# Ternary feed-forward block: scaling and low parts of the second token half on VectorE instead of GpSimd, at the end of the first half

## The chip, the cores and the metric

One core of one Trainium2 chip (trn2) runs the whole program. The time is that of the device, in microseconds from one launch, as the median of several runs. The profiler's span, from the first to the last instruction, is about 2 us shorter than the time of the execution that it belongs to.

## The reference

Two post-norm decoder layers on 8 sequences of 100 tokens with 512 channels (800 tokens). Each layer has a mixer or attention, a cross attention on 361 context rows and a feed-forward block, each followed by x = layernorm(x + block(x)). The change lies in the feed-forward block of the first layer, whose weights are made ternary:

```python
def _L0_ffn_ref(x, w1, b1, w2, b2):
    def _bit_quant(w):
        scale = jnp.maximum(jnp.mean(jnp.abs(w)), EPS)
        w_ternary = jnp.clip(jnp.round(w / scale), -1.0, 1.0)
        return w + jax.lax.stop_gradient(w_ternary - w)
    w1q = _bit_quant(w1)
    w2q = _bit_quant(w2)
    h = jnp.einsum('bsd,fd->bsf', x, w1q) + b1
    h = jax.nn.gelu(h, approximate=False)
    return jnp.einsum('bsf,df->bsd', h, w2q) + b2

def _layernorm(x, axis=-1, eps=1e-05):
    m = jnp.mean(x, axis=axis, keepdims=True)
    v = jnp.var(x, axis=axis, keepdims=True)
    return (x - m) / jnp.sqrt(v + eps)
...
    x = _layernorm(x + _L0_xattn_ref(x, ctx_2048, ...), axis=-1)
    x = _layernorm(x + _L0_ffn_ref(x, L0_ffn_w1, L0_ffn_b1, L0_ffn_w2, L0_ffn_b2), axis=-1)
```

w1 is 2048 x 512 and w2 is 512 x 2048.

## The kernel before

The program is a chain of stages, each a block with one instruction list per engine and a barrier of all engines behind it. Activations lie in `X` as 128 partitions x C = 4 channel groups x 800 tokens. In the ternary stage (`ternary_ffn_stage`, L1198) the tokens are done in two halves of 400 (`at` = 0 and 1), and each half in FC = 16 steps `j`, one per 128 hidden channels. The order on each engine is written out by hand, and semaphores tie the engines together.

- **TensorE** (L1284 to L1305): `hidden(at, j)` is 8 matmuls (L1255; 4 channel groups, high and low part of X), `down(at, j)` is 8 matmuls (L1268; 4 output groups, high and low part of the hidden values). The list runs hidden 0, hidden 1, then down j and hidden j + 2 in turn. So down j stands behind hidden j + 1. In the first half hidden j waits for `up_ready` and down j for `down_ready`, as the ternary weights are made while the half runs; every down waits for `h2_ready`.
- **ScalarE** (L1318 to L1341): in each step Gelu out of PSUM into `hid` (L1322) and its high part (Copy, L1325). Between the steps stand pieces of the layer norm and the high parts of the second half (`high_part`, L1309).
- **VectorE** (L1368 to L1405): in each step the low part `h2` (L1381, one 128x400 tensor_tensor), and, in the first half only, the ternary weights of a later step: `ternary_up(j + 2)` and `ternary_down(j + 1)`, each a tensor_scalar of 128x512 (L1350, L1359) and a scalar_tensor_tensor of 128x512 (L1352, L1361). In the first half the layer norm of the second half's tokens is done in between: `nrm.center(1, i)` in steps 0 and 1, `nrm.invert(1, i)` (a reciprocal of 128x200, L195) in steps 6 and 8. At the end of the first half VectorE waits for `y_all` and adds the four outputs into X (`add_out`, L1365), which `down(1, 0)` waits for.
- **GpSimd** (L1408): has six instructions in this stage. They are the second half's `nrm.apply(1, i)` (L204, two tensor_tensor of 128x800: X = centred values x 1/std) and its low parts, four tensor_tensor of 128x400 (L1413), each behind the high part that ScalarE made. `hidden(1, 0)` waits for all of them through `part_lo`.

The low parts of the first half are made by VectorE at the stage's head, in the same form (L1373). SyncE's list fetches the ternary weights' raw values into a ring of 8 places and is told by `up_ready` and `down_ready` when a place is free.

Of the kernel before, what the change touches and what calls it, by code (L numbers as in the profile page):

```python
# [17 lines left out]
ACT = mybir.ActivationFunctionType  # L18
ALU = mybir.AluOpType
# [5 lines left out]
C = D // P  # L25
# [415 lines left out]
FC = F // P  # L441
# [756 lines left out]
def ternary_ffn_stage(nc, core, a, tern, early):  # L1198


    X, psum = core.X, core.psum
    LEAD, nrm, half = 2, tern.nrm, core.half
    with ExitStack() as ctx:
        def sb(name, shape, dt=F32):
            return ctx.enter_context(nc.sbuf_tensor(f"tf_{name}", shape, dt))
# [7 lines left out]
        parts = sb("parts", [P, 2, C, N], F32R)  # L1213
        S_ = {n: core.sem(f"tf_{n}") for n in (
            "part_hi", "part_lo", "last_mean", "up_low", "down_low", "up_ready", "down_ready", "h_mm", "hid_ready", "hi_ready", "h2_ready", "y_all", "y_out")}
        core.held += [*tern.sems, *tern.raw_in]
        block = ctx.enter_context(nc.Block())

        def piece(j):

            r = j % tern.SLOTS
            whole = tern.first[:, r, :] if r < tern.LEAD else ring[:, r - tern.LEAD, :]
            return whole, whole[:, 0:D].rearrange("p (c o) -> p c o", c=C), whole[:, D:2 * D]

        def half_of(h):
            return slice(h * HALF, (h + 1) * HALF)

        def quarter(i):
            return slice(i * QUARTER, (i + 1) * QUARTER)

        def cols(j):
            return slice(j * P, (j + 1) * P)

        def last_mean_at(i):
            return psum[:, (4, 7)[i], quarter(i)]

        @block.sync
        def _(sp):
            for j in range(tern.LEAD, FC):
                if j >= tern.SLOTS:  # L1240
                    sp.wait_ge(S_["up_ready"], j - tern.SLOTS + 1)
                    sp.wait_ge(S_["down_ready"], j - tern.SLOTS + 1)
                tern.fetch(sp, a, j, piece(j)[0])
            early.fetch(sp, a)
# [61 lines left out]

        @block.scalar
        def _(act):
            def high_part(at, c):  # L1309
                act.wait_ge(nrm.normed, 2 * at + 2)  # L1310
                act.activation(parts[:, 0, c, half_of(at)], X[:, c, half_of(at)], ACT.Copy).then_inc(S_["part_hi"], 1)

            act.wait_ge(nrm.normed, 1)
            act.activation(parts[:, 0, :, quarter(0)], X[:, :, quarter(0)], ACT.Copy)
            act.wait_ge(nrm.normed, 2)
            for c in range(C):
                act.activation(parts[:, 0, c, quarter(1)], X[:, c, quarter(1)], ACT.Copy).then_inc(S_["part_hi"], 1)
            for at in range(2):  # L1318
                for j in range(FC):
                    m, r = at * FC + j, j % 2  # L1320
                    act.wait_ge(S_["h_mm"], m + 1)
                    act.activation(hid[:, r, :], psum[:, 4 + r, 0:HALF], ACT.Gelu,  # L1322
                                   bias=core.param("b1", j)).then_inc(S_["hid_ready"], 1)
                    act.wait_ge(S_["hid_ready"], m + 1)
                    act.activation(h2[:, r, 0, :], hid[:, r, :], ACT.Copy).then_inc(S_["hi_ready"], 1)  # L1325
                    if not at and j in (1, 2):
                        nrm.square(act, 1, j - 1)
                    if not at and j == 4:
                        nrm.root(act, 1, 0)
                        nrm.root(act, 1, 1)  # L1330
                    if not at and j in (10, 11, 12, 13):
                        high_part(1, j - 10)
                    if at and j in (3, 4):
                        nrm.square(act, 2, j - 3)
                    if at and j == 7:
                        nrm.root(act, 2, 0)
                        nrm.root(act, 2, 1)
            for i in range(2):
                nrm.square(act, 3, i)
            for i in range(2):  # L1340
                nrm.root(act, 3, i)  # L1341

        @block.vector
        def _(dve):
            def ternary_up(j):
                _, up, _ = piece(j)
                dve.wait_ge(tern.raw_in[j % tern.SLOTS], 16 * (j // tern.SLOTS + 1))
                if j:
                    dve.wait_ge(S_["up_ready"], j)
                dve.tensor_scalar(low_up[:, :, :], up, half[:, 1:2], None, ALU.is_lt).then_inc(S_["up_low"], 1)  # L1350
                dve.wait_ge(S_["up_low"], j + 1)
                dve.scalar_tensor_tensor(w_up[:, :, cols(j)], up, half[:, 0:1], low_up[:, :, :],  # L1352
                                         ALU.is_gt, ALU.subtract).then_inc(S_["up_ready"], 1)

            def ternary_down(j):
                _, _, down = piece(j)
                if j:
                    dve.wait_ge(S_["down_ready"], j)
                dve.tensor_scalar(low_down[:, :], down, half[:, 3:4], None, ALU.is_lt).then_inc(S_["down_low"], 1)  # L1359
                dve.wait_ge(S_["down_low"], j + 1)  # L1360
                dve.scalar_tensor_tensor(w_down[:, j, :], down, half[:, 2:3], low_down[:, :],  # L1361
                                         ALU.is_gt, ALU.subtract).then_inc(S_["down_ready"], 1)

            def add_out(at, c, tok):
                dve.scalar_tensor_tensor(X[:, c, tok], psum[:, c, tok.start - at * HALF:tok.stop - at * HALF],  # L1365
                                         core.param("b2", c), X[:, c, tok], ALU.add, ALU.add).then_inc(S_["y_out"], 1)

            nrm.apply(dve, 0, 1)  # L1368
            dve.wait_ge(tern.half_ready, 4)
            ternary_up(0)  # L1370
            for c in range(C):
                dve.wait_ge(S_["part_hi"], c + 1)
                dve.tensor_tensor(parts[:, 1, c, half_of(0)], X[:, c, half_of(0)], parts[:, 0, c, half_of(0)],  # L1373
                                  ALU.subtract).then_inc(S_["part_lo"], 1)
            ternary_up(1)
            ternary_down(0)
            for at in range(2):
                for j in range(FC):
                    m, r = at * FC + j, j % 2
                    dve.wait_ge(S_["hi_ready"], m + 1)  # L1380
                    dve.tensor_tensor(h2[:, r, 1, :], hid[:, r, :], h2[:, r, 0, :], ALU.subtract).then_inc(S_["h2_ready"], 1)  # L1381
                    if not at and j + LEAD < FC:
                        ternary_up(j + LEAD)
                    if not at and j + 1 < FC:
                        ternary_down(j + 1)
                    if not at and j in (0, 1):
                        nrm.center(dve, 1, j)
                    if not at and j in (6, 8):
                        nrm.invert(dve, 1, (j - 6) // 2)
                    if at and j in (3, 4):  # L1390
                        nrm.center(dve, 2, j - 3)
                    if at and j in (8, 9):
                        nrm.scale(dve, 2, j - 8)
                dve.wait_ge(S_["y_all"], at + 1)
                if at == 0:
                    for c in range(C):
                        add_out(0, c, half_of(0))
            for i in range(2):
                for c in range(C):
                    add_out(1, c, nrm.tok(3, i))  # L1400
            for i in range(2):
                tok = nrm.tok(3, i)
                dve.wait_ge(S_["last_mean"], i + 1)
                dve.tensor_tensor(nrm.cen[:, :, tok], X[:, :, tok], last_mean_at(i).unsqueeze(1).broadcast_to([P, C, QUARTER]),
                                  ALU.subtract).then_inc(nrm.cen_ready, 1)  # L1405

        @block.gpsimd
        def _(pool):  # L1408
            for i in range(2):
                nrm.apply(pool, 1, i)  # L1410
            for c in range(C):
                pool.wait_ge(S_["part_hi"], C + c + 1)
                pool.tensor_tensor(parts[:, 1, c, half_of(1)], X[:, c, half_of(1)], parts[:, 0, c, half_of(1)],  # L1413
                                   ALU.subtract).then_inc(S_["part_lo"], 1)


FLT_EPS = float(np.finfo(np.float32).eps)
# [1468 lines left out]
```

## Time and profile before

| what | value |
|---|---|
| median of 3 runs | 2252.76 us (2252.47 to 2253.65) |
| the profiled execution's own time | 2251.19 us |
| its span | 2249.3 us |
| TensorE busy | 2154.1 us, 96% |
| VectorE busy | 1475.3 us, 66% |
| ScalarE busy | 1177.7 us, 52% |
| GpSimd busy | 478.6 us, 21% |
| mean granted TensorE clock | 0.988 |

Busy shares are means over stages with different limits. The ternary stage takes from 1219.6 to about 1349 us of the span, its first half up to about 1286. A start time less the start time of the row before it on the same engine is what an instruction costs its queue; the duration printed in a row is a little longer, since an instruction's end overlaps the next one's beginning. What ended an idle time stands in brackets behind a row.

### The profile page before, as it was taken

The numbers are of one execution on the slowest core, as the hardware profiler recorded it, in microseconds if no ns is written. First come the engines' busy times: TensorE is split into PE (matmuls) and PEld (weight loads), VectorE is DVE, ScalarE is ACT, GpSimd is POOL, SyncE is SP. The second block draws the span as 40 slices with busy tenths as digits, with TensorE's granted clock in tenths as the row PEclk, the third lists the DMA queues.
The fourth block names the chain that finished last, engine by engine and source line by source line (L and its number), as shares of the span: only waits on it lengthen the run. The fifth ranks groups of instructions, "written<-read, shape, count | busy, mean of one in ns | idle before, by whom it ended". The sixth has DMA issues, their size and how long they took to land. (4 is left out here: it accounts for less than half of the span.)

```text
span 2249.3 us, 35511 instructions
## 1 busy us (share of the span) xinstructions
PE 2154.1 (96%) x13284; PEld 1689.8 (75%) x13304; DVE 1475.3 (66%) x4005; ACT 1177.7 (52%) x3020; POOL 478.6 (21%) x445
## 2 busy tenths in 40 slices
PE   9998999999999999999998899999998999997998
PEld 6644788888888888888886785665655885665997
DVE  2385777787777777687667837565565557883545
ACT  2053667576767667676554344453533346771332
POOL 1210121221221222221120102232253000221443
PEclk9999999999999999999999999999999999999999
DMA  6013110111111111100102203223222320003200
GB/s 250 8 62 117 38 34 13 38 38 36 39 39 36 38 39 36 39 11 8 57 6 75 89 1 143 103 80 117 89 78 90 134 80 20 2 1 131 94 1 29
DMA packets 44387, 131.66 MB, mean 59 GB/s; under 512 B 6663, under 2 KB 21799, under 8 KB 40247
## 3 DMA queue, kind: packets, MB, share of 16 engines
q1 hardware_dynamic: 32408, 108.32, 13.2%
q0 software_dynamic: 2304, 12.58, 1.4%
q10 hardware_dynamic: 9504, 8.50, 1.3%
q8 instruction: 105, 1.72, 0.3%
q14 instruction: 66, 0.54, 0.1%
HBM read 108.84 MB, written 20.15 MB: 57 GB/s over the span
## 5 line engine op out<-in xcount | busy, mean ns | idle before, releaser
L784 PE MATMUL psum<-la_w_both,context 128*128 128x256 f32 (+1 forms) x1536 | 343.6, 380 | 0.0
L784 PEld LDWEIGHTS psum<-la_w_both,context 128*128 128x128 f32 (+1 forms) x1536 | 277.2, 184 | 44.9
L770 PE MATMUL psum<-qa_w,room 128*100 128x256 bf16 (+1 forms) x3072 | 266.8, 247 | 3.1 <-PEq L60 3.1
L770 PEld LDWEIGHTS psum<-qa_w,room 128*100 128x100 bf16 x3072 | 255.8, 126 | 4.1 <-issue 4.0
L894 ACT ACTIVATE qa_prob<-psum,qa_nm 100x361 f32<-100x361 f32 x128 | 72.0, 562 | 168.0 <-DVE qa_nm L1031 168.0
L1143 POOL TENSOR_TENSOR qa_w<-qa_w_raw,qa_w 128x768 bf16<-128x768 f32 x28 | 46.0, 1644 | 370.7 <-DVE qa_w L973 370.7
L2579 ACT ACTIVATE it_prob<-psum,it_nm 100x257 f32<-100x257 f32 (+1 forms) x256 | 101.9, 413 | 41.5 <-DVE it_nm L2610 41.4
L993 DVE BATCH_NORM_STATS2 qa_st<-psum 100x6 f32<-100x128 f32 x320 | 69.7, 284 | 78.6 <-PE psum L770 78.6
L1149 POOL TENSOR_TENSOR qa_o<-la_w_qt,qa_o 128x512 fp32r<-128x512 f32 x32 | 40.6, 1269 | 350.4 <-DVE qa_o L981 350.4
L1022 DVE TENSOR_SCALAR qa_nrm_t<-psum,qa_mv,qa_sd 100x128 f32<-100x128 f32 x320 | 107.8, 403 | 2.4
L1476 PE MATMUL psum<-gf_parts,gf_w 128*128 128x400 f32 x512 | 101.3, 352 | 8.3 <-DMA gf_w<-gf_ternary 8.3
L841 PE MATMUL psum<-qa_catq,qa_o 128*128 128x400 f32 x512 | 108.2, 354 | 0.8 <-POOL qa_catq L1159 0.8
L1476 PEld LDWEIGHTS psum<-gf_parts,gf_w 128*128 128x128 f32 x512 | 96.0, 193 | 9.3 <-DMA gf_w<-gf_ternary 9.0
L806 PE MATMUL psum<-qa_kxT,qa_qT 128*100 128x361 f32 x256 | 98.8, 468 | 1.3 <-ACT qa_qT L888 1.3
L1961 PE MATMUL psum<-la_oT,la_w_vo 128*128 128x400 f32 x256 | 93.6, 521 | 3.1 <-issue 2.9
L894 ACT ACT_TABLE_LOAD x64 | 82.1, 1283 | 24.9 <-ACT qa_size L927 13.4
L1035 DVE RECIPROCAL qa_rsum<-qa_sums 100x4 f32<-100x4 f32 x64 | 11.4, 178 | 125.3 <-ACT qa_prob L896 125.3
L841 PEld LDWEIGHTS psum<-qa_catq,qa_o 128*128 128x128 f32 x512 | 89.4, 189 | 1.2 <-POOL qa_catq L1159 0.9
L1916 PE MATMUL psum<-X,la_w_q 128*128 128x400 f32 x256 | 89.9, 499 | 0.2
L1155 POOL TENSOR_TENSOR qa_yt<-qa_yb,qa_ym 128x400 f32<-128x400 bf16 x64 | 60.2, 941 | 114.1 <-DVE qa_ym L1064 114.1
L1961 PEld LDWEIGHTS psum<-la_oT,la_w_vo 128*128 128x128 f32 x256 | 50.6, 199 | 44.7 <-issue 13.7
L900 ACT ACT_TABLE_LOAD x64 | 82.1, 1283 | 1.1
(354 smaller groups left out, 5036.4 us busy)
## 6 DMA issues: line engine op xcount, KB each, us to landing
qa_w_raw<-in_qa_w SPq DMA_DIRECT2D x8, 1536.0 KB, 15.3
la_gf_raw<-in_gf_w SPq DMA_DIRECT2D x16, 768.0 KB, 4.9
gf_w<-gf_ternary SPq DMA_DIRECT2D x4, 3072.0 KB, 21.9
qa_piece<-in_tf_pieces ACTq DMA_DIRECT2D x64, 128.0 KB, 2.1
la_w_qt<-in_qa_o SPq DMA_DIRECT2D x8, 1024.0 KB, 5.2
gf_ternary<-la_gf_made POOLq DMA_DIRECT2D x8, 768.0 KB, 3.7
gf_ternary<-gf_last_made POOLq DMA_DIRECT2D x8, 768.0 KB, 3.9
context<-in_context SPq DMA_DIRECT2D x8, 722.0 KB, 12.4
```

The source lines that it names most:

```text
L770: mm = pe.matmul(psum[0:T, 2 + at // 512, at % 512:at % 512 + width], xq[:, kind, k, b * T:(b + 1) * T], w3[:, s, part, k, at:at + width], ...
L784: mm = pe.matmul(psum[0:rows, i // 2, (i % 2) * 256:(i % 2) * 256 + 256], ctxT[:, k, b * TC + t0:b * TC + t0 + rows], kv_raw[:, s, k, :], ...
L806: pe.matmul(psum[0:T, 6 + h, 0:TC], qT[:, 2 + h, :], kxT[:, :], start=True, stop=True)
L841: mm = pe.matmul(psum[:, bank, 0:HALF], o2[:, part, j, c * P:(c + 1) * P], catq[:, quad, j, :], start=(part == 0 and j == 0), stop=(part = ...
L894: act.activation(prob[:, h, 0:TC], psum[0:T, 6 + h, 0:TC], ACT.Exp, scale=QK_SCALE, bias=nm[:, h:h + 1], accum_out=sums[:, h:h + 1])
L900: act.activation(spare[:, :], core.eps[1.0], ACT.Sqrt)
L993: dve.bn_stats(st[0:T, 3 + i, :], psum[0:T, bank, c0:c0 + P]).then_inc(S_["tok_st"], 1)
L1022: last = dve.tensor_scalar(nrm_t[:, i, :], psum[0:T, bank, c0:c0 + P], mv[0:T, 3 + i, 0:1], sd[0:T, 3 + i:4 + i], ALU.subtract, ALU.mult)
L1476: mm = pe.matmul(hidden_bank(m, u), w[:, j, u, k * P:(k + 1) * P], parts[:, part, k, half_of(half)], start=(part == 0 and k == 0), stop=(p ...
L1916: mm = pe.matmul(psum[:, bank, 0:HALF], (w_q if kind == "q" else w_rot)[:, k, i * P:(i + 1) * P], X[:, k, cols(h)], start=(k == 0), stop=( ...
L1961: mm = pe.matmul(psum[:, 6 + i % 2, 0:HALF], w_vo[:, j, c * P:(c + 1) * P], oT[:, j, cols(h)], start=(j == 0), stop=(j == 3))
L2579: last = act.activation(prob[:, r, j, x0:x1], psum[0:T, 2 * r + j, x0:x1], ACT.Exp, scale=IT_SCALE, bias=nm[:, r, at:at + 1], accum_out=su ...
```

## The change

The GpSimd block of the stage is gone. VectorE does `nrm.apply(1, 0)` in step 13 and `nrm.apply(1, 1)` in step 14 of the first half, ahead of the next step's `h2`, and the four low parts behind the `h2` of step 15, ahead of its wait for `y_all`. The two reciprocals move from steps 6 and 8 to steps 7 and 10. ScalarE makes the high parts of the second half in steps 14 (first quarter, one 128x800 activation) and 15 (second quarter, four of 128x200), where it made one of 128x400 in each of steps 10 to 13. `QUARTER` is N // 4 = 200 tokens. Helpers replace code that was written out twice.

```diff
         @block.scalar
         def _(act):
-            def high_part(at, c):
-                act.wait_ge(nrm.normed, 2 * at + 2)
-                act.activation(parts[:, 0, c, half_of(at)], X[:, c, half_of(at)], ACT.Copy).then_inc(S_["part_hi"], 1)
-
-            act.wait_ge(nrm.normed, 1)
-            act.activation(parts[:, 0, :, quarter(0)], X[:, :, quarter(0)], ACT.Copy)
-            act.wait_ge(nrm.normed, 2)
-            for c in range(C):
-                act.activation(parts[:, 0, c, quarter(1)], X[:, c, quarter(1)], ACT.Copy).then_inc(S_["part_hi"], 1)
+            def high_parts(at, i):
+
+                tok = nrm.tok(at, i)
+                act.wait_ge(nrm.normed, 2 * at + i + 1)
+                if i == 0:
+                    act.activation(parts[:, 0, :, tok], X[:, :, tok], ACT.Copy)
+                    return
+                for c in range(C):
+                    act.activation(parts[:, 0, c, tok], X[:, c, tok], ACT.Copy).then_inc(S_["part_hi"], 1)
+
+            high_parts(0, 0)
+            high_parts(0, 1)
...
-                    if not at and j in (10, 11, 12, 13):
-                        high_part(1, j - 10)
+                    if not at and j in (14, 15):
+                        high_parts(1, j - 14)
...
+            def low_parts(at):
+                for c in range(C):
+                    dve.wait_ge(S_["part_hi"], at * C + c + 1)
+                    dve.tensor_tensor(parts[:, 1, c, half_of(at)], X[:, c, half_of(at)], parts[:, 0, c, half_of(at)],
+                                      ALU.subtract).then_inc(S_["part_lo"], 1)
...
-            for c in range(C):
-                dve.wait_ge(S_["part_hi"], c + 1)
-                dve.tensor_tensor(parts[:, 1, c, half_of(0)], X[:, c, half_of(0)], parts[:, 0, c, half_of(0)],
-                                  ALU.subtract).then_inc(S_["part_lo"], 1)
+            low_parts(0)
...
-                    if not at and j in (6, 8):
-                        nrm.invert(dve, 1, (j - 6) // 2)
+                    if not at and j in (7, 10):
+                        nrm.invert(dve, 1, (j - 7) // 3)
+                    if not at and j in (13, 14):
+                        nrm.apply(dve, 1, j - 13)
+                    if not at and j == FC - 1:
+                        low_parts(1)
...
-        @block.gpsimd
-        def _(pool):
-            for i in range(2):
-                nrm.apply(pool, 1, i)
-            for c in range(C):
-                pool.wait_ge(S_["part_hi"], C + c + 1)
-                pool.tensor_tensor(parts[:, 1, c, half_of(1)], X[:, c, half_of(1)], parts[:, 0, c, half_of(1)],
-                                   ALU.subtract).then_inc(S_["part_lo"], 1)
```

Instructions, as they stand on each engine. VectorE, the last steps of the first half, before (`tf_h` is h2, `tf_low_up` and `tf_low_down` the first halves of making weights, `room` the centred values):

```order
2033 L1361 SCALAR_TENSOR_TENSOR tf_w_down<-tf_ring,tf_half,tf_low_down 128x512
2034 L1381 TENSOR_TENSOR tf_h<-tf_hid,tf_h 128x400
2035 L1359 TENSOR_SCALAR tf_low_down<-tf_ring,tf_half 128x512
2036 L1361 SCALAR_TENSOR_TENSOR tf_w_down<-tf_ring,tf_half,tf_low_down 128x512
2037 L1381 TENSOR_TENSOR tf_h<-tf_hid,tf_h 128x400
2038 L1365 SCALAR_TENSOR_TENSOR X<-psum,params,X 128x400 x4
```

The same place of the changed program:

```order
2033 L1364 SCALAR_TENSOR_TENSOR tf_w_down<-tf_ring,tf_half,tf_low_down 128x512
2034 L204 TENSOR_TENSOR X<-room,norm_std 128x4x200
2035 L1387 TENSOR_TENSOR tf_h<-tf_hid,tf_h 128x400
2036 L1362 TENSOR_SCALAR tf_low_down<-tf_ring,tf_half 128x512
2037 L1364 SCALAR_TENSOR_TENSOR tf_w_down<-tf_ring,tf_half,tf_low_down 128x512
2038 L204 TENSOR_TENSOR X<-room,norm_std 128x4x200
2039 L1387 TENSOR_TENSOR tf_h<-tf_hid,tf_h 128x400
2040 L1370 TENSOR_TENSOR tf_parts<-X,tf_parts 128x400 x4
2041 L1374 SCALAR_TENSOR_TENSOR X<-psum,params,X 128x400 x4
```

Two scalings now stand ahead of the last two `h2`, and four low parts between the last `h2` and the additions.

ScalarE, steps 13 to 15 of the first half, before:

```order
1436 L1322 ACTIVATE tf_hid<-psum,params 128x400
1437 L1325 ACTIVATE tf_h<-tf_hid 128x400
1438 L1311 ACTIVATE tf_parts<-X 128x400
1439 L1322 ACTIVATE tf_hid<-psum,params 128x400
1440 L1325 ACTIVATE tf_h<-tf_hid 128x400
1441 L1322 ACTIVATE tf_hid<-psum,params 128x400
1442 L1325 ACTIVATE tf_h<-tf_hid 128x400
```

and in the changed program, steps 14 and 15 and the first of the second half:

```order
1435 L1325 ACTIVATE tf_hid<-psum,params 128x400
1436 L1328 ACTIVATE tf_h<-tf_hid 128x400
1437 L1314 ACTIVATE tf_parts<-X 128x4x200
1438 L1325 ACTIVATE tf_hid<-psum,params 128x400
1439 L1328 ACTIVATE tf_h<-tf_hid 128x400
1440 L1317 ACTIVATE tf_parts<-X 128x200 x4
1441 L1325 ACTIVATE tf_hid<-psum,params 128x400
1442 L1328 ACTIVATE tf_h<-tf_hid 128x400
```

The high parts moved from between steps 10 to 14 to behind steps 14 and 15. TensorE's and SyncE's lists hold the same instructions in the same order.

## Rows read from the trace of the kernel before

**Rows 1.** The page, part 1: busy time, share of the span, instructions.

```profile
PE 2154.1 (96%) x13284; PEld 1689.8 (75%) x13304; DVE 1475.3 (66%) x4005; ACT 1177.7 (52%) x3020; POOL 478.6 (21%) x445
```

**Rows 2.** Busy time by stretch: start:end, length, engines' busy us, granted clock, DMA share, GB/s.

```profile
1223.00:1286.00 63.00, 54.11 (x267) 47.90 (x266) 54.87 (x84) 24.67 (x42) 8.88 (x6) 0.99 0.37 134
...
1270.00:1280.00 10.00, 8.83 (x46) 7.83 (x45) 9.79 (x15) 4.15 (x8) 2.87 (x3) 1.00 0.00 0
...
1286.00:1340.00 54.00, 52.62 (x273) 49.27 (x272) 17.78 (x26) 23.08 (x38) 0.00 (x0) 1.00 0.00 1
...
1247.07:1283.68 36.61, 30.05 (x152) 26.97 (x152) 35.50 (x51) 13.01 (x24) 8.88 (x6) 1.00 0.25 94
```

**Rows 3.** Who waited for whom, 1215 to 1290 us: total, times, longest.

```profile
PE psum L1268 <- DVE tf_h L1381: 7.1, 12, 1.0
```

**Rows 4.** Timeline of VectorE, step 3 and head of step 4: start, duration, instruction.

```profile
1237.24 0.57 DVE L1381 TENSOR_TENSOR tf_h<-tf_hid,tf_h 128x400 fp32r<-128x400 f32 x1
1237.72 0.48 DVE L1350 TENSOR_SCALAR tf_low_up<-tf_ring,tf_half 128x512 bf16<-128x512 f32 x1
1238.24 0.75 DVE L1352 SCALAR_TENSOR_TENSOR tf_w_up<-tf_ring,tf_half,tf_low_up 128x512 fp32r<-128x512 f32 x1
...
1240.09 0.57 DVE L1381 TENSOR_TENSOR tf_h<-tf_hid,tf_h 128x400 fp32r<-128x400 f32 x1
```

**Rows 5.** Timeline of TensorE, step 4.

```profile
1238.02 1.61 PE L1268 MATMUL psum<-tf_h,tf_w_down 128*128 128x400 f32 x8
1239.47 1.62 PE L1255 MATMUL psum<-tf_parts,tf_w_up 128*128 128x400 f32 x8
```

**Rows 6.** Timeline of VectorE, steps 5 to 14: first h2, a reciprocal, the lengthened instructions.

```profile
1247.07 0.58 DVE L1381 TENSOR_TENSOR tf_h<-tf_hid,tf_h 128x400 fp32r<-128x400 f32 x1 [4.05 <-ACT tf_h L1325]
...
1252.79 1.39 DVE L195 RECIPROCAL norm_std<-norm_std 128x200 f32<-128x200 f32 x1
1254.10 0.51 DVE L1381 TENSOR_TENSOR tf_h<-tf_hid,tf_h 128x400 fp32r<-128x400 f32 x1
1254.53 2.12 DVE L1350 TENSOR_SCALAR tf_low_up<-qa_w_raw,tf_half 128x512 bf16<-128x512 f32 x1
...
1265.96 1.27 DVE L1359 TENSOR_SCALAR tf_low_down<-qa_w_raw,tf_half 128x512 bf16<-128x512 f32 x1
...
1277.29 1.43 DVE L1361 SCALAR_TENSOR_TENSOR tf_w_down<-tf_ring,tf_half,tf_low_down 128x512 fp32r<-128x512 f32 x1
```

**Rows 7.** Timeline of GpSimd, three of its six instructions in the stage.

```profile
1254.26 2.11 POOL L204 TENSOR_TENSOR X<-room,norm_std 128x800 f32<-128x800 f32 x1 [46.89 <-DVE norm_std L195]
...
1265.62 1.32 POOL L1413 TENSOR_TENSOR tf_parts<-X,tf_parts 128x400 fp32r<-128x400 f32 x1 [0.65 <-ACT tf_parts L1311]
...
1277.10 1.08 POOL L1413 TENSOR_TENSOR tf_parts<-X,tf_parts 128x400 fp32r<-128x400 f32 x1 [2.46 <-ACT tf_parts L1311]
```

**Rows 8.** Timeline of VectorE at the stage's head: the same operations for the first half.

```profile
1219.59 0.99 DVE L204 TENSOR_TENSOR X<-room,norm_std 128x800 f32<-128x800 f32 x1 [1.06 <-PEq L60]
1220.50 0.48 DVE L1350 TENSOR_SCALAR tf_low_up<-qa_w_raw,tf_half 128x512 bf16<-128x512 f32 x1
...
1221.68 2.02 DVE L1373 TENSOR_TENSOR tf_parts<-X,tf_parts 128x400 fp32r<-128x400 f32 x4
```

**Rows 9.** Timeline of ScalarE: four small high parts; a 128x800 activation and the Gelu behind.

```profile
1220.61 1.15 ACT L1317 ACTIVATE tf_parts<-X 128x200 fp32r<-128x200 f32 x4 [0.18 <-DVE X L204]
...
1234.50 0.87 ACT L169 ACTIVATE room<-room 128x800 f32<-128x800 f32 x1 [1.82 <-DVE room L163]
1235.28 0.58 ACT L1322 ACTIVATE tf_hid<-psum,params 128x400 f32<-128x400 f32 x1
```

**Rows 10.** Timeline of VectorE at the end of the first half: h2 15, add_out, h2 of the second half.

```profile
1283.68 0.57 DVE L1381 TENSOR_TENSOR tf_h<-tf_hid,tf_h 128x400 fp32r<-128x400 f32 x1 [0.43 <-ACT tf_h L1325]
1286.07 2.26 DVE L1365 SCALAR_TENSOR_TENSOR X<-psum,params,X 128x400 f32<-128x400 f32 x4 [1.82 <-PE psum L1268]
1288.73 0.58 DVE L1381 TENSOR_TENSOR tf_h<-tf_hid,tf_h 128x400 fp32r<-128x400 f32 x1 [0.40 <-ACT tf_h L1325]
```

**Rows 11.** Who waited for whom from 1340 us to the end: the wait for a DMA.

```profile
PE psum L1476 <- DMA gf_w<-gf_ternary: 8.3, 1, 8.3
```

## The prediction

> **What bounds the kernel now.** I read the page's busy shares first, then busy time by stretch, then the waits, then the timelines. The shares say TensorE, 96% [rows 1], but they are a mean over stages. The two halves of the ternary stage differ: in the first one TensorE is busy 54.11 of 63 us and VectorE 54.87, in the second 52.62 of 54 and 17.78 [rows 2]. So TensorE paces the second half and something else the first. The waits name it: TensorE's down matmuls waited 7.1 us, 12 times, for VectorE's h2 [rows 3].
>
> The timelines say why. A plain step of the first half costs VectorE 1240.09 - 1237.24 = 2.85 us (one h2, two tensor_scalar of 0.48, two scalar_tensor_tensor of 0.75) [rows 4], and TensorE 2 x 1.45 = 2.90 [rows 5]. They are level, so whatever is added to VectorE's list in this half becomes its length. From the h2 of step 5, at 1247.07, to the h2 of step 15, at 1283.68, VectorE is busy 35.50 of 36.61 us [rows 2, 6, 10]: it is the bound there, and all that the change touches on VectorE ahead of step 15's h2 lies in that stretch.
>
> In it six VectorE instructions are longer than their kind, each beside one of GpSimd's six. The tensor_scalar at 1254.53 takes 2.12 us where 0.48 is usual, beside GpSimd's scaling of 1254.26 to 1256.37; the one at 1265.96 takes 1.27 beside a low part up to 1266.94; the scalar_tensor_tensor at 1277.29 takes 1.43 for 0.75 beside a low part up to 1278.18 [rows 4, 6, 7]. VectorE's ends come 0.3 to 0.5 us behind GpSimd's. Each of these three stands for two in the trace, alike within 0.02 us. The excess is 2 x 1.64 + 2 x 0.79 + 2 x 0.68 = **6.22 us**. That is what I take GpSimd's six instructions to cost the stage. The Trainium skill (SBUF — State Buffer, Who interferes with whom) has a rule for this: the two engines share one pair of ports, a VectorE tensor_scalar that uses both ports or a VectorE operation on two SBUF inputs excludes GpSimd, and the later one stands still until the earlier is done. By that rule, the trace agrees, all six lengthenings go when GpSimd has nothing to do.
>
> **The change, part by part.** Counted from step 5's h2 to step 15's on VectorE:
>
> - Removed: the 6.22 us.
> - Reciprocals from steps 6 and 8 to 7 and 10: two before, two after, each 1254.10 - 1252.79 = 1.31 us of VectorE's queue [rows 6], both inside the stretch. Nothing. Their users come later than before (steps 13 and 14), so no one waits for them.
> - Two scalings on VectorE, in steps 13 and 14: the same operation at the stage's head costs the queue 1220.50 - 1219.59 = 0.91 us [rows 8]. Plus 2 x 0.91 = **1.82**, on the path.
> - The wait of 0.43 us for ScalarE ahead of step 15's h2 [rows 10] goes: the second scaling fills it. Step 14 has no ternary_up left, so VectorE needs 0.48 for h2 and 1.19 for the one pair of weight instructions (half of 2.85 - 0.48, [rows 4]), 1.67 in all, plus 0.91: 2.58 between the two h2. ScalarE has to be ready by then: it waits for the first scaling, which ends 0.08 us after step 14's h2 starts (0.99 long, spaced 0.91), makes the first high part (1235.28 - 1234.50 = 0.78 to the next issue), Gelu (0.58) [rows 9] and a Copy that I put at the same, so it is ready about 2.1 us behind that h2: 0.4 us to spare. Saved **0.43**.
>
> Whole stretch after: 9 plain steps of 2.855 (25.70), the short one 1.67, two reciprocals at 1.25 (1.31 less the 0.06 by which the h2 behind one is shorter, 0.43 for 0.49 in [rows 4, 6]), two scalings 1.82: 31.69 us, for 36.61. **4.9 us less.** By the differences alone it is 6.22 + 0.43 - 1.82 = 4.83; the 0.09 between the two is the hand-over behind a blocked instruction.
>
> Behind step 15's h2:
>
> - High parts of the second quarter on ScalarE: four take 1.15 us [rows 9] and start when step 15's Copy and the second scaling are done, about when this h2 starts. ScalarE then idles until hidden(1, 0); nothing waits but the low parts.
> - Four low parts on VectorE, 2.02 us for all [rows 8], start 0.49 behind h2's start and end at +2.5. Before, VectorE waited there for TensorE's last down and began add_out at 1286.07 - 1283.68 = +2.39, so low parts fit but for 0.1 us. add_out takes 2.26 and the next h2 starts at +5.05 after an idle of 0.40 [rows 10], which covers the 0.1. TensorE's hidden(1, 0) starts at about +2.2 and needs the fourth low part only 6 matmuls later, at 0.18 each (2.90 / 16, [rows 5]), +3.3. Cost nothing; without that cover, up to 2.02.
> - The old high parts between steps 10 to 13 were ScalarE work beside its idle time. Nothing. SyncE waits for up_ready and down_ready, which come earlier; its transfers move along.
> - The second half is TensorE's (52.62 of 54 [rows 2]) and unchanged, so the 4.9 us pass through it and the barrier to the end.
>
> **Sum.** The profiled execution took 2251.19 us for a span of 2249.3; it should read about 2246.3. The median of runs shown is 2252.76, 1.6 above the profiled one; less 4.9 it is **2247.9 us**. The line of 0.2%, which is about what a measurement can tell from no change, lies at 4.5 us, 2248.25: the forecast is only 0.4 us beyond it.
>
> **Rivals.**
>
> 1. *The end of the half takes some back.* Low parts stand ahead of add_out, and down(1, 0) waits for add_out; ScalarE's Gelu of step 15 stands behind a wait for VectorE that was not there. For it: the margins are 0.3 us (0.40 less 0.1) and 0.4 us. Against: each was worked out to hold. With the low parts wholly exposed, 4.9 - 2.02 = 2.9 us gained: 2249.9.
> 2. *The lengthened instructions are not GpSimd's doing* (their raw weights arrive by DMA in the same stretch). Then the 6.22 stays, VectorE gets 1.82 more and loses its wait of 0.43: +1.39, **2254.2**, slower than before, and 2256.2 with the low parts exposed. It decides if less than 1.39 of the 6.22 goes. Against: all six sit beside a GpSimd instruction, and the one at 1277.29 stands where the DMA engines' share is 0.00 [rows 2]. The Trainium skill (Perfetto Trace Analysis, Optimizing Scalar/DVE Operations) speaks against this change in general: where VectorE is saturated, work may go to ScalarE or even to GpSimd. Taken alone it gives this rival's time; the same passage warns of the port the two share.
> 3. *TensorE becomes the bound earlier and gives more.* It is idle 36.61 - 30.05 = 6.56 us of the stretch [rows 2]. That is the most that can go: 2246.2. Against: VectorE's list of 31.69 us is still longer than TensorE's 30.05.
> 4. *The gain is lost downstream.* The one wait for a DMA behind the stage is 8.3 us for the last stage's weights [rows 11]. If that transfer started at a fixed time the gain would end there: 2252.8. Against: it is issued behind the barriers, so it moves along.
>
> That the change does not do what it says I leave out: the lists show each move, and GpSimd's block is empty.
>
> **Chances.** Forecast 0.74, rival 1 0.12, rival 2 0.06, rival 3 0.04, rival 4 0.04. Within the forecast the time may lie either side by the spread of runs, 1.2 us; as it is 0.4 beyond the line, I count three in four of it as faster: 0.56, with rival 3 0.60. Rivals 1 and 4, the rest of the forecast and nearly all of rival 2 are within 0.2%: 0.38. Rival 2's upper end is 1.1 us under the line of 2257.3, which a run's spread can reach: 0.02 slower. Range: 1.1 below the forecast, 2246.8, and up to rival 1's end with 0.3 of spread, 2250.2. It leaves out rival 2, rival 4 and a part of rival 3.
>
> **What would show it.** Right: no tensor_scalar of the stage above 0.5 us and no scalar_tensor_tensor above 0.76; two scalings of 0.99 on VectorE; step 5's h2 to step 15's 31.7 us; no idle ahead of step 15's h2; from there to the next half's first h2 5.05 as before; TensorE's wait for h2 down from 7.1. Wrong: long tensor_scalar without GpSimd (rival 2), an idle of VectorE ahead of step 15's h2 or more than 5.1 us behind it (rival 1), a wait of the last stage that grew by 5 us (rival 4).

## The result, and the profile after

| what | before | changed |
|---|---|---|
| median, timed side by side (16 runs each) | 2253.53 us | 2247.12 us |
| ratio of the two, 95% interval | | 0.9975 [0.9966, 0.9983] |
| the profiled execution's own time | 2251.19 us | 2247.96 us |
| its span | 2249.3 us | 2245.9 us |
| GpSimd busy | 478.6 us | 469.5 us |
| VectorE busy | 1475.3 us | 1473.1 us |
| mean granted TensorE clock | 0.988 | 0.987 |

The change made the kernel faster by 0.25% here. In a second comparison, further down, the same two kernels stood at 0.9992 [0.9983, 1.0001]; why so small a difference scatters so much is taken up there. The stage itself hardly scatters (its stretch took 31.68 and 31.69 us in two profiles of the changed kernel), and it is read from the trace.

Busy time of the changed kernel, from step 5's h2 to step 15's (start:end, length, busy TensorE, weight loads, VectorE, ScalarE, GpSimd, granted clock, DMA share, GB/s), the counterpart of the last row of [rows 2]:

```profile
1247.38:1279.06 31.68, 28.75 (x152) 27.41 (x152) 31.00 (x52) 11.94 (x21) 0.00 (x0) 1.00 0.29 108
```

31.68 us for 36.61. VectorE is still busy nearly throughout, and TensorE does its 152 matmuls of the stretch in less time. Its waits in the stage (total, times, longest), for the 7.1 us of [rows 3]:

```profile
PE psum L1268 <- DVE tf_h L1387: 5.9, 9, 1.0
```

VectorE's timeline around step 8 and at the end of the half, for [rows 6] and [rows 10]:

```profile
1257.27 0.51 DVE L1387 TENSOR_TENSOR tf_h<-tf_hid,tf_h 128x400 fp32r<-128x400 f32 x1
1257.69 0.47 DVE L1353 TENSOR_SCALAR tf_low_up<-qa_w_raw,tf_half 128x512 bf16<-128x512 f32 x1
...
1275.59 0.98 DVE L204 TENSOR_TENSOR X<-room,norm_std 128x800 f32<-128x800 f32 x1
1276.49 0.57 DVE L1387 TENSOR_TENSOR tf_h<-tf_hid,tf_h 128x400 fp32r<-128x400 f32 x1
...
1278.16 0.98 DVE L204 TENSOR_TENSOR X<-room,norm_std 128x800 f32<-128x800 f32 x1
1279.06 0.57 DVE L1387 TENSOR_TENSOR tf_h<-tf_hid,tf_h 128x400 fp32r<-128x400 f32 x1
1279.58 2.03 DVE L1370 TENSOR_TENSOR tf_parts<-X,tf_parts 128x400 fp32r<-128x400 f32 x4
1281.53 2.26 DVE L1374 SCALAR_TENSOR_TENSOR X<-psum,params,X 128x400 f32<-128x400 f32 x4
1284.11 0.57 DVE L1387 TENSOR_TENSOR tf_h<-tf_hid,tf_h 128x400 fp32r<-128x400 f32 x1 [0.33 <-ACT tf_h L1328]
```

The tensor_scalar behind the reciprocal took 2.12 us and takes 0.47. The two scalings take 0.98 each and cost the queue 0.90. There is no idle ahead of step 15's h2 at 1279.06 (it was 0.43). The low parts end where add_out begins, and the next half's h2 comes 5.05 us behind step 15's, as before; the idle ahead of it went from 0.40 to 0.33.

ScalarE at the same place:

```profile
1276.60 0.87 ACT L1314 ACTIVATE tf_parts<-X 128x800 fp32r<-128x800 f32 x1 [1.63 <-DVE X L204]
1277.38 0.58 ACT L1325 ACTIVATE tf_hid<-psum,params 128x400 f32<-128x400 f32 x1
1277.99 0.54 ACT L1328 ACTIVATE tf_h<-tf_hid 128x400 fp32r<-128x400 f32 x1
```

The Gelu of step 15 stands behind the wait for the scaling, and its Copy ends at 1278.53, 0.5 us before VectorE asks for it.

Where the time went then: the same matmul groups start 4.6 to 4.7 us earlier at the stage's end (last L1280 at 1339.8 for 1344.5), having started 0.3 us later at the stage's head (first L1268 at 1227.8 for 1227.5). At the span's end only 3.4 of that are left. The gain did not meet a new wait: TensorE's longest one behind the stage, for the last stage's weights, is 8.3 us in both kernels [rows 11]. TensorE's clock fell at other places of the later stages. The first matmul of three later blocks started 4.6, 1.6 and 3.3 us earlier (1345.87 for 1350.48, 1731.03 for 1732.67, 1860.01 for 1863.35), and over the windows of 10 us from 1350 on, what the granted clock lacked to full adds up to 20.4 us in the changed kernel and 18.8 before. Of the changed kernel, then of the kernel before, two stretches of the latent attention stage:

```profile
1430.00:1440.00 10.00, 9.29 (x21) 5.15 (x21) 3.83 (x5) 2.89 (x3) 0.00 (x0) 0.70 0.86 338
...
1610.00:1620.00 10.00, 7.93 (x27) 4.04 (x27) 4.68 (x10) 6.53 (x13) 0.00 (x0) 1.00 0.35 123
```

```profile
1430.00:1440.00 10.00, 7.93 (x28) 4.32 (x28) 4.71 (x8) 6.14 (x12) 0.00 (x0) 1.00 0.42 158
...
1610.00:1620.00 10.00, 7.34 (x33) 4.03 (x32) 4.63 (x11) 7.60 (x23) 0.00 (x0) 0.84 0.07 20
```

The changed kernel ran part of 1430 to 1440 at 1.2 GHz (0.70 of full on the mean), where the other had 2.4 GHz throughout; around 1610 it was the other way round.

### The profile page after: what moved, and what is told of

Read it like the earlier page. It is cut to its first block and busy times, and to the rows that moved or that the text cites. A ratio compares the mean times of both kernels' runs of the same rounds, so it can differ in the third digit from the quotient of the medians.

```text
span 2245.9 us, 35532 instructions
## 1 busy us (share of the span) xinstructions
PE 2154.9 (96%) x13304; PEld 1690.1 (75%) x13304; DVE 1473.1 (66%) x4011; ACT 1176.5 (52%) x3021; POOL 469.5 (21%) x439
```

## The experiments

The measure is the time between the h2 starts of steps 5 and 15 on VectorE, "the stretch": 36.61 us before, 31.68 changed. An edit is one of the changed kernel, unless "against before" stands beside it. Experiments 1, 3, 5 and 6 and the second profile of 8 are single executions; as a kernel's times spread over some 10 us, only their stretch is read.

**1. The reciprocals back in their steps.**

```diff
-                    if not at and j in (7, 10):
-                        nrm.invert(dve, 1, (j - 7) // 3)
+                    if not at and j in (6, 8):
+                        nrm.invert(dve, 1, (j - 6) // 2)
```

> The changed kernel with its two reciprocals back in steps 6 and 8. My theory (VectorE's list is serial from step 5's h2 to step 15's, so where a reciprocal stands in it is worth nothing): 31.7 us between these two h2 starts, as in the changed kernel (31.68), and the same time within 0.5 us. Rival (the gain came in part from moving them): 0.5 to 1.3 us more in that stretch.

Measured: stretch 31.68 us, the same to the last digit. VectorE's list has no idle time there, and to move the reciprocals within it cost nothing. The one execution took 2249.59 us, 2.5 above the changed kernel's median; its trace had a stretch at 1.2 GHz ahead of the ternary stage already (1200 to 1210 us, granted 0.66), so its h2 of step 5 came at 1250.74 for 1247.38.

**2. Six GpSimd instructions that nobody needs.**

```diff
+        idle_out = sb("idle_out", [P, 8, 100])
...
+        @block.gpsimd
+        def _(pool):
+            ones, done = core.ones[:, 0:100].unsqueeze(1), 0
+            triggers = [(nrm.inv_ready, 3, 8), (nrm.inv_ready, 4, 8)] + [(S_["up_ready"], 13 + c, 4) for c in range(C)]
+            for n, (sem, at, width) in enumerate(triggers):
+                pool.wait_ge(sem, at)
+                if n:
+                    pool.wait_ge(S_["idle"], n)
+                pool.tensor_tensor(idle_out[:, 0:width, :], ones.broadcast_to([P, width, 100]),
+                                   ones.broadcast_to([P, width, 100]), ALU.mult).then_inc(S_["idle"], 1)
```

> The changed kernel, with six GpSimd tensor_tensor added at the places where the old ones ran (two of 128x800 behind the reciprocals, four of 128x400 behind the ternary weights of steps 12 to 15). They read a constant and write a tile that nobody reads; VectorE keeps all its work and nobody waits for GpSimd. My theory (the lengthened VectorE instructions are GpSimd's doing): two tensor_scalar of about 2.1 us and four more instructions lengthened by 0.6 to 0.9 us; the stretch from step 5's h2 to step 15's grows from 31.7 to 37 to 38 us, the time by 5 to 6.2 us over the changed kernel, so it is as slow as the kernel before or slower by 1 us. Rival (the arrival of the raw weights by DMA, or the instructions' place, lengthened them): 31.7 us, as fast as the changed kernel.

Measured: stretch 36.10 us, ratio to the kernel before 0.9995 [0.9982, 1.0007]. Nobody waits for the added work, and still 4.4 of the 4.9 us gained are gone. GpSimd's first instruction and VectorE's lengthened ones in this kernel's timeline:

```profile
1260.53 1.73 POOL L1426 TENSOR_TENSOR tf_idle_out<-ones 128x800 f32<-128x800 f32 x1 [50.20 <-DVE norm_std L195]
```

```profile
1260.79 1.74 DVE L1354 TENSOR_SCALAR tf_low_up<-qa_w_raw,tf_half 128x512 bf16<-128x512 f32 x1
1271.88 1.74 DVE L1354 TENSOR_SCALAR tf_low_up<-tf_ring,tf_half 128x512 bf16<-128x512 f32 x1
1273.65 1.23 DVE L1356 SCALAR_TENSOR_TENSOR tf_w_up<-tf_ring,tf_half,tf_low_up 128x512 fp32r<-128x512 f32 x1
1275.31 1.22 DVE L1365 SCALAR_TENSOR_TENSOR tf_w_down<-tf_ring,tf_half,tf_low_down 128x512 fp32r<-128x512 f32 x1
```

Six lengthenings, 2 x 1.26 + 4 x 0.47 = 4.4 us, which is the stretch's growth of 4.42. The expectation of 37 to 38 was too high, because GpSimd's instruction is shorter on this constant: 1.73 us where the real scaling took 2.11 [rows 7]. This is the experiment that settles the cause. It keeps the raw weights' DMA (about 3.4 MB in the stretch, by GB/s times length, in this kernel as in the changed one) and the order on VectorE as they were, and only adds GpSimd.

**3. Memsets in their place.**

```diff
+            n = 0
+            triggers = [(nrm.inv_ready, 3, 3), (nrm.inv_ready, 4, 3)] + [(S_["up_ready"], 13 + c, 2) for c in range(C)]
+            for sem, at, count in triggers:
+                pool.wait_ge(sem, at)
+                for _ in range(count):
+                    if n:
+                        pool.wait_ge(S_["idle"], n)
+                    pool.memset(idle_out[:, :, :], 0.0).then_inc(S_["idle"], 1)
+                    n += 1
```

> As the kernel with six added GpSimd tensor_tensor, but with memsets of 128x800 in their place (three in a row behind each reciprocal, two behind each of the four weights), which write and read nothing. If GpSimd's reads are what excludes VectorE: no VectorE instruction is lengthened, 31.7 us for the stretch. If any GpSimd access excludes it: tensor_scalar and scalar_tensor_tensor both lengthened, 35 us or more. If, as the Trainium skill (SBUF — State Buffer, Who interferes with whom) states, a write-only GpSimd instruction excludes only VectorE's two-port forms: tensor_scalar lengthened by up to a memset's time, scalar_tensor_tensor (0.75) and tensor_tensor never. In numbers from this case's rows I expect the last, at 1 to 4 us more than 31.7.

Measured: stretch 34.40 us, 2.72 more. The longer tensor_scalar and the scalar_tensor_tensor, in the timeline and in the groups by form from 1240 to 1282 us (busy, mean ns | idle):

```profile
1259.80 1.11 DVE L1363 TENSOR_SCALAR tf_low_down<-qa_w_raw,tf_half 128x512 bf16<-128x512 f32 x1
...
1270.53 1.10 DVE L1363 TENSOR_SCALAR tf_low_down<-tf_ring,tf_half 128x512 bf16<-128x512 f32 x1
```

```profile
L1365 DVE SCALAR_TENSOR_TENSOR tf_w_down<-tf_ring,tf_half,tf_low_down 128x512 fp32r<-128x512 f32 x9 | 6.8, 752 | 0.3
...
L1356 DVE SCALAR_TENSOR_TENSOR tf_w_up<-tf_ring,tf_half,tf_low_up 128x512 fp32r<-128x512 f32 x7 | 5.3, 751 | 0.2
```

Only tensor_scalar is lengthened, seven of them, to between 0.62 and 1.11 us, 2.71 in all; scalar_tensor_tensor stays at 0.75 beside the same memsets, while it took 1.22 beside GpSimd operations that read. The Trainium skill (SBUF — State Buffer, Who interferes with whom) states just this difference: a VectorE instruction with two SBUF inputs collides with a GpSimd instruction that reads SBUF, not with one that only writes it. The trace agrees.

**4. Half of the change: only the low parts on VectorE** (against before).

```diff
+                    if not at and j == FC - 1:
+                        for c in range(C):
+                            dve.wait_ge(S_["part_hi"], C + c + 1)
+                            dve.tensor_tensor(parts[:, 1, c, half_of(1)], X[:, c, half_of(1)], parts[:, 0, c, half_of(1)],
+                                              ALU.subtract).then_inc(S_["part_lo"], 1)
...
             for i in range(2):
                 nrm.apply(pool, 1, i)
-            for c in range(C):
-                pool.wait_ge(S_["part_hi"], C + c + 1)
-                pool.tensor_tensor(parts[:, 1, c, half_of(1)], X[:, c, half_of(1)], parts[:, 0, c, half_of(1)],
-                                   ALU.subtract).then_inc(S_["part_lo"], 1)
```

> The kernel before with one part of the change: the four low parts go to VectorE behind step 15's h2; the two scalings stay on GpSimd in their place, the high parts in steps 10 to 13. My theory: the four smaller lengthenings go (2 x 0.79 + 2 x 0.68 = 2.94 us), the two of 1.64 stay, the low parts are hidden behind TensorE's last down: 33.7 us for the stretch where the kernel before has 36.61, and 2.9 us less in time. Rival (the low parts cost their 2.02 us on the path): 0.9 us less. Rival (the lengthenings come from elsewhere): no less, 2 us more.

Measured: stretch 33.88 us (33.7 expected), 5.07 to the next half's h2, ratio 0.9987 [0.9977, 0.9997], which is 2.9 us. Two tensor_scalar of 2.13 us are left. The 0.2 us that is short of the expectation is idle time: ahead of step 15's h2 VectorE now waits 0.62 us for ScalarE, where it was 0.43, since it arrives sooner.

**5. The other half: only the scalings on VectorE** (against before).

```diff
-                        nrm.invert(dve, 1, (j - 6) // 2)
+                        nrm.scale(dve, 1, (j - 6) // 2)
...
-            for i in range(2):
-                nrm.apply(pool, 1, i)
```

> The kernel before with the other part of the change alone: the two scalings on VectorE, each behind its reciprocal in steps 6 and 8; the low parts stay on GpSimd. My theory: the two lengthenings of 1.64 go, two scalings of 0.91 come, the four smaller lengthenings stay: 36.61 - 3.28 + 1.82 = 35.1 us for the stretch (up to 0.4 less if VectorE no longer idles ahead of step 15's h2). With the 2.7 us of the low parts' experiment it would make up the change's gain but for the idle time. Rival (scalings cost VectorE more than the waiting did): 36.6 or more.

Measured: stretch 35.87 us, a gain of 0.74 for the 1.5 expected. Two things were missed. A scaling right behind its reciprocal makes the step 0.1 us longer (5.19 for the 5.08 of the sum), as it waits for the reciprocal's end. And the four lengthenings that stay are 3.05 us and not 2.94, one now on an h2 (1.43 us). In addition TensorE has longer gaps, and its clock fell within the stretch. TensorE's timeline there, and the granted clock of the stretch behind the gap; then the one h2 of VectorE that had to wait behind it:

```profile
1256.77 1.72 PE L1268 MATMUL psum<-tf_h,tf_w_down 128*128 128x400 f32 x8 [1.94 <-DVE tf_h L1381]
...
1264.82 2.09 PE L1268 MATMUL psum<-tf_h,tf_w_down 128*128 128x400 f32 x8 [1.95 <-DVE tf_h L1381]
1266.70 2.91 PE L1255 MATMUL psum<-tf_parts,tf_w_up 128*128 128x400 f32 x8
```

```profile
1265.00:1270.00 5.00, 5.00 (x20) 4.67 (x21) 4.86 (x9) 0.35 (x1) 1.07 (x1) 0.66 0.00 0
```

```profile
1270.84 0.57 DVE L1381 TENSOR_TENSOR tf_h<-tf_hid,tf_h 128x400 fp32r<-128x400 f32 x1 [0.18 <-ACT tf_h L1325]
```

After two gaps of 1.9 us the clock of TensorE went down to 1.2 GHz for a part of these 5 us (0.66 on the mean), and eight matmuls took 2.91 us for 1.62. In the kernel before the longest gap in these steps was 1.1 us and the clock stayed at 1.00. The missing gain can be read off VectorE's list. The sum gives 35.15 us, 0.7 less than measured: 0.2 are the two scalings that wait for their reciprocals, 0.1 the longer lengthenings, 0.1 that an h2 costs the queue 0.49 behind a scaling and 0.43 behind a reciprocal, and 0.3 are the clock's, in the step before the h2 at 1270.84, which took 3.12 us for 2.86 because ScalarE waited for the slow matmuls and VectorE for ScalarE.

**6. Low parts made twice,** to see how much room they have.

```diff
+        twice = sb("twice", [P, C, HALF], F32R)
...
+                        for c in range(C):
+                            dve.wait_ge(S_["part_hi"], C + c + 1)
+                            dve.tensor_tensor(twice[:, c, :], X[:, c, half_of(1)], parts[:, 0, c, half_of(1)], ALU.subtract)
                         low_parts(1)
```

> The changed kernel with four more tensor_tensor of 128x400 ahead of the four low parts behind step 15's h2 (into a tile that nobody reads). My theory (the four low parts are hidden with about 0.3 us to spare): the stretch up to step 15's h2 stays at 31.7, and from there to the next half's first h2 it is 6.6 to 6.8 us for 5.05, as 2.0 us more find 0.33 of idle. Rival (they are on the path already): 7.1. Rival (there is far more room): 5.05 to 5.5.

Measured: stretch 31.67 us, then 6.58 us to the next half's h2 for 5.05. So 1.95 us more of VectorE work cost 1.53: the low parts were hidden, with 0.4 us to spare.

```profile
1278.31 0.57 DVE L1388 TENSOR_TENSOR tf_h<-tf_hid,tf_h 128x400 fp32r<-128x400 f32 x1
1278.83 2.03 DVE L1402 TENSOR_TENSOR tf_twice<-X,tf_parts 128x400 fp32r<-128x400 f32 x4
1280.78 2.03 DVE L1371 TENSOR_TENSOR tf_parts<-X,tf_parts 128x400 fp32r<-128x400 f32 x4
1282.72 2.26 DVE L1375 SCALAR_TENSOR_TENSOR X<-psum,params,X 128x400 f32<-128x400 f32 x4
1284.89 0.57 DVE L1388 TENSOR_TENSOR tf_h<-tf_hid,tf_h 128x400 fp32r<-128x400 f32 x1
```

**7. The changed kernel once more, and weights made ahead.** With GpSimd out of the way VectorE's list is still the bound, and it idles 4 us ahead of step 5's h2 (the bracket in [rows 6]), while ScalarE loads tables and takes square roots. Three weight pairs can be made there.

```diff
-                    if not at and j + LEAD < FC:
-                        ternary_up(j + LEAD)
-                    if not at and j + 1 < FC:
-                        ternary_down(j + 1)
+                    if not at:
+                        for u in {4: (6, 7, 8), 5: (9,), 6: (10,), 7: (), 8: (11,), 9: (12,), 10: ()}.get(j, (j + LEAD,)):
+                            if u < FC:
+                                ternary_up(u)
+                        for d in {4: (5, 6), 13: ()}.get(j, (j + 2,) if 4 < j < 13 else (j + 1,)):
+                            if d < FC:
+                                ternary_down(d)
```

> The changed kernel as it is, timed beside the kernel with weights made ahead. Stretch 31.68 us; 4.9 us less than the kernel before in the stage, ratio 0.9978, within what other stages' clock scatters.

> The changed kernel, with three of VectorE's weight pairs (1.19 us each) made early, in the idle time of 4.05 us that VectorE has ahead of step 5's h2: ternary_up 7 and 8 and ternary_down 6 in step 4, and steps 7, 10 and 13, which hold a reciprocal or a scaling, are short of one pair each. My theory (VectorE's list bounds steps 5 to 15, TensorE's is next at 19 groups of 1.46 us and ScalarE's 1.15 behind): the stretch from step 5's h2 to step 15's falls from 31.68 to 28.3 to 28.6 us, where TensorE and ScalarE set it, 3.2 us less than the changed kernel and 8.1 less than the kernel before, ratio 0.9964. Rival (TensorE bounds already, or the raw weights are not there so early): 31 us or more, no gain.

Measured: the changed kernel again 31.69 us for the stretch, ratio 0.9992 [0.9983, 1.0001]; with weights ahead 28.39 us and ratio 0.9970 [0.9960, 0.9980], median 2244.86 us beside 2248.32 for the changed kernel and 2250.32 for the kernel before. It beats both. The expected ratio of 0.9978 for the changed kernel lies outside its interval, though its stretch is to 0.01 us what was expected; what scatters lies in other stages and is taken up below. With weights ahead TensorE sets the pace: in its stretch TensorE is busy 27.76 of 28.39 us:

```profile
1249.83:1278.22 28.39, 27.76 (x152) 27.63 (x152) 27.64 (x48) 12.13 (x22) 0.00 (x0) 1.00 0.41 138
```

**8. The same weights ahead, but with GpSimd's work as before** (against before; the edit is that of 7).

> The kernel before, GpSimd's six instructions included, with the same three weight pairs made early. My theory (with 6.2 us of lengthening VectorE still bounds the steps, so the order alone does not free it): 36.61 less 3.57 and, with no idle ahead of step 15's h2, less 0.43: 32.6 us, up to 33.3 if a lengthened instruction falls into a short step; 3.5 to 4 us less than the kernel before and about 4.2 more than the kernel with weights ahead and no GpSimd. Rival (with room in VectorE's list GpSimd's work is hidden again): 29 us, as without GpSimd.

> The kernel before with three weight pairs ahead once more, for a second profile. In the first one the granted clock of TensorE fell inside the stretch (0.83 over 1270 to 1280 us, 1.00 in every other kernel's). If that fall is a chance of the execution: 33 to 34 us for the stretch and a clock of 1.00. If it comes from the idle times that GpSimd causes in this order: 35.8 us and the same fall again.

Measured: 35.84 and 35.82 us, ratio 1.0006 [0.9993, 1.0019]. My expectation of 32.6 to 33.3 us was wrong. Of the two cases that I had set down for the second profile, the second came true: the fall of the clock was no chance, it came in both profiles at the same step. TensorE's timeline in the second one:

```profile
1264.68 1.72 PE L1268 MATMUL psum<-tf_h,tf_w_down 128*128 128x400 f32 x8 [0.94 <-DVE tf_h L1381]
1266.24 1.62 PE L1255 MATMUL psum<-tf_parts,tf_w_up 128*128 128x400 f32 x8
1269.97 3.03 PE L1268 MATMUL psum<-tf_h,tf_w_down 128*128 128x400 f32 x8 [2.11 <-DVE tf_h L1381]
```

The reciprocals stand in steps 6 and 8 here and the short steps are 7 and 10, so in step 9 a reciprocal's delay meets a lengthened tensor_scalar (2.13) and another of 1.27. TensorE waits 2.11 us, its clock falls (granted 0.68 over 1270 to 1275 us), and later VectorE idles 1.12 and 1.62 us for ScalarE, which waits for TensorE. My expectation counted VectorE's list alone. So three pairs made ahead save 3.3 us without GpSimd and 0.8 with it.

**The scatter between runs.** Within one kernel's runs the time goes with the mean granted clock. In the table, the mean time of the runs that showed a mean clock (rounded to 0.001 as recorded), with their number; the kernel before is from two of the comparisons:

```
clock   before        changed       weights ahead
0.984   2255.8 (6)    2253.3 (1)    -
0.985   -             2253.1 (2)    -
0.986   2254.3 (10)   2249.5 (4)    2245.8 (5)
0.987   2252.0 (5)    2247.7 (14)   2243.7 (4)
0.988   2250.6 (11)   2244.6 (3)    2240.9 (1)
0.989   2248.5 (12)   2242.5 (3)    -
```

At an equal clock the change is worth 4.3 to 6 us, and 2.5 at 0.984, where the changed kernel has a single run. A fit of all timed runs of these comparisons (the six kernels with ten runs or more), with one constant for each kernel and one slope, gives 1.85 us per 0.001 of clock and 4.5 us between before and changed (2252.0 and 2247.5, each known to 0.2 us), then 3.8 us more with weights ahead. All 60 runs of the kernel before have a mean of 2251.96, all 27 of the changed one 2247.62: 4.3 us, 0.19%. The ratio of 0.9975 stands on the good side of that and 0.9992 on the bad side. The stage's 4.9 us would be 0.22%.

## Why the prediction was right

The measured 2247.12 us lies 0.8 below the forecast of 2247.9, within the range. By its steps:

- *VectorE is the bound from step 5 to 15, and its list is serial there.* Right. The list was added up to 31.69 us and the trace has 31.68; a second profile has 31.69.
- *6.22 us are GpSimd's.* Right, and shown. Six GpSimd instructions without a user brought 4.4 of them back, with each VectorE instruction lengthened beside its own. Rival 2 (arrival of raw weights) is out: the same 3.4 MB came in the stretch of the changed kernel without a lengthening and in this one with six. Taking away the four low parts alone took away exactly the four smaller lengthenings.
- *Reciprocals cost nothing by moving.* Right, to 0.01 us.
- *Two scalings at 0.91.* They cost 0.90. The wait of 0.43 went, as said.
- *ScalarE ready 0.4 us before it is needed.* It was 0.5. *Low parts hidden with 0.3 us to spare.* It was 0.33 by the idle and 0.4 by doubling them. Rival 1 is out.
- *TensorE as the next bound (rival 3).* It is idle 2.9 of 31.68 us. It did not bind, but it is near: with weights ahead it does, at 28.39.
- *The 4.9 us pass to the end (rival 4 otherwise).* Right as to waits: no wait of TensorE behind the stage grew by more than 0.1 us, the one for the last stage's weights is 8.3 us as before. What the prediction left out is TensorE's clock in those stages. It counted 1.2 us of spread from three runs; over all runs the changed kernel's times reach from 2242 to 2253. In the profiled pair 1.2 us of the gain went to clock that fell at other places. In the 16 runs of the result the means lie 5.7 us apart, 0.8 more than the stage gives; the clocks of the kernel before are not on record for these runs, so that the clock is the reason is not shown there.
- *The sum.* That the median came within 0.8 us of the forecast is in part luck. The medians lie 6.4 us apart in the result and 2.0 in the second comparison, while the stage gives 4.9 in either profile of the changed kernel.
- *The chances.* The forecast lay 0.4 us beyond the line of 0.2%, and the runs fall on both sides of it: 0.25% in the result, 0.08% in the second comparison, 0.19% over all runs.

## What to carry to other kernels

Before work goes to GpSimd because VectorE is busy, look for VectorE instructions that are longer than their kind beside GpSimd's: if VectorE is the bound there, each costs its surplus. Here GpSimd's 8.9 us cost VectorE 6.2, and VectorE did the same work in 3.8, of which 2.0 fell into a wait that it had anyway. Where an engine's list is the bound, add it up instruction by instruction from start to start; and move work from a full step into the engine's own idle time before looking for another engine. A difference of 0.2% is read from the stage's trace and from runs at an equal granted clock, not from one pair of medians.

## What had not been expected of the hardware

- TensorE's clock can fall at gaps in steps that ran at 2.4 GHz in every other kernel here. Two gaps of 1.9 us, or one of 0.94 and one of 2.11 five microseconds later, were followed by matmuls at 1.2 GHz (granted 0.66 and 0.68 over 5 us); with gaps up to 1.2 us it did not happen in these steps. The length of a gap alone does not decide it: ahead of 1430 us, in the latent attention stage, both kernels have gaps of 0.6 to 0.7 us, and the changed one fell (0.70 over 1430 to 1440) where the other stayed at 1.00. A stall on VectorE can so cost more than its length.
- The same program's mean granted clock differs between executions from 0.984 to 0.989, and its time by 11 us with it.
- GpSimd's tensor_tensor of 128x800 takes 1.73 us when both inputs are one small constant repeated and 2.11 on two tensors, and VectorE's surplus shrinks with it, from 1.64 to 1.26 us.
